# The last feed-forward of a twelve-stage decoder: every token through every expert, or tokens scattered to slots by expert

## The reference

```python
def _swiglu(flat, gate_w, up_w, down_w):
    return (silu(flat @ gate_w.T) * (flat @ up_w.T)) @ down_w.T
flat = x.reshape(-1, 128)                       # 1024 tokens, normalized
out = _swiglu(flat, shared_gate, shared_up, shared_down)      # 512 hidden channels
probs = softmax(flat @ router_w.T)              # 7 routed experts
top_vals, top_idx = top_k(probs, 2)
top_vals = top_vals / (top_vals.sum(-1) + 1e-9)
combine = sum(one_hot(top_idx, 7) * top_vals[..., None], axis=1)
for e in range(7):
    routed += combine[:, e:e+1] * _swiglu(flat, routed_gate[e], routed_up[e], routed_down[e])
return out + routed
```

## Time and profile before

| | |
|---|---|
| median of three runs | 1525.89 us (1523.6 to 1533.68) |
| profiled execution | 1525.1 us, span 1523.3 us |
| PE / DVE / ACT / POOL busy | 87% / 58% / 39% / 29% of the span |
| mean granted PE clock | 0.873 |
| last stage, first instruction to output issued | 1343.6 to 1520.2 us |
| HBM read / written | 91.15 MB / 1.59 MB |

### The profile page before, as it was taken

The page is one execution under the profiler, slowest core; times in us unless marked ns, Lnnn a source line. Parts: engine busy times, 40 slices in busy tenths (PEclk is TensorE's granted clock), DMA queues, the critical chain, the costliest instruction groups (busy, mean ns, idle before and its releaser), DMA issues. The chain is left out here.

```text
span 1523.3 us, 31521 instructions
## 1 busy us (share of the span) xinstructions
PE 1323.7 (87%) x12561; PEld 905.6 (59%) x12569; DVE 885.7 (58%) x1642; ACT 595.9 (39%) x1343; POOL 447.9 (29%) x251
## 2 busy tenths in 40 slices
PE   3579889989879898979997967979998998689998
PEld 1268878888745554556773554546674545356665
DVE  7488888888656645663335844861125767453333
ACT  2434444444325434514332711744435654122221
POOL 5099989999454031010002101110001010000000
PEclk9657888887877899979997977989997979789999
DMA  2197677877510000001110000000100000011110
GB/s 96 44 239 215 204 205 208 211 210 207 193 28 2 2 0 1 2 14 31 39 28 1 2 1 1 1 29 28 41 14 1 2 1 1 1 42 42 41 41 14
DMA packets 47097, 94.46 MB, mean 62 GB/s; under 512 B 4848, under 2 KB 9216, under 8 KB 46720
## 3 DMA queue, kind: packets, MB, share of 16 engines
q1 hardware_dynamic: 46976, 92.76, 21.8%
HBM read 91.15 MB, written 1.59 MB: 61 GB/s over the span
## 5 line engine op out<-in xcount | busy, mean ns | idle before, releaser
L618 ACT ACTIVATE shifted_a<-scores,nmax_a 128x128 f32<-128x128 f32 x768 | 208.6, 387 | 87.9 <-DVE nmax_a L584 86.5
L1078 PE MATMUL decay<-delta,A_pairs 32*128 32x127 f32 x2048 | 176.3, 333 | 47.3 <-DVE small_pack L1172 19.5
L1153 ACT ACTIVATE decay<-decay 128x1016 f32<-128x1016 f32 x128 | 128.7, 1010 | 193.8 <-PE decay L1078 193.8
L1410 DVE SCALAR_TENSOR_TENSOR X<-Y,comb_e,X 128x128 f32<-128x128 f32 x256 | 72.1, 345 | 212.0 <-PE Y L1352 212.0
L1334 PE MATMUL G<-XNT,W_e 128*128 128x512 f32 x384 | 193.3, 614 | 1.6 <-DMA W_e<-L3f_w 1.1
L1078 PEld LDWEIGHTS decay<-delta,A_pairs 32*128 32x128 f32 x2048 | 153.7, 233 | 67.7 <-DVE small_pack L1172 24.7
L1352 PEld LDWEIGHTS Y<-W_e,hid_e 128*128 128x128 f32 x1536 | 179.1, 192 | 23.0 <-issue 19.1
L584 DVE TENSOR_REDUCE nmax_a<-scores 128x4 f32<-128x512 f32 x192 | 123.8, 686 | 110.4 <-PE scores L523 108.1
L325 POOL TENSOR_TENSOR rstd<-ve,neghalf 128x4 f32<-128x4 f32 x30 | 30.6, 1022 | 520.0 <-DVE ve L311 520.0
L1352 PE MATMUL Y<-W_e,hid_e 128*128 128x128 f32 x1536 | 179.2, 275 | 0.0
L1377 ACT ACTIVATE hid_e<-G,W_e 128x512 f32<-128x512 f32 x128 | 88.0, 687 | 127.4 <-PE G L1334 122.6
(11 more groups left out here) (329 smaller groups left out, 2016.9 us busy)
## 6 DMA issues: line engine op xcount, KB each, us to landing
pos_bias<-du_rows SPq DMA_DIRECT2D x72, 256.0 KB, 4.8
XN<-du_rows SPq DMA_DIRECT2D x38, 256.0 KB, 4.7
XNT<-du_rows SPq DMA_DIRECT2D x38, 256.0 KB, 4.8
O<-du_rows SPq DMA_DIRECT2D x36, 256.0 KB, 4.7
masked_cos<-du_rows SPq DMA_DIRECT2D x36, 256.0 KB, 4.7
masked_sin<-du_rows SPq DMA_DIRECT2D x36, 256.0 KB, 4.7
W_e<-L3f_w SPq DMA_DIRECT2D x8, 768.0 KB, 4.2
small_pack<-small SPq DMA_DIRECT2D x1, 4517.0 KB, 14.4
```

What stands on the lines that cost most here:

```text
L618: t = nc.scalar.activation(shifted[u % 4][:, j, :], scores[u % 4][:, j, :], ACT.Exp, scale=-1.0, bias=nmax[:, u % 4, j:j + 1])
L1078: t = nc.tensor.matmul(decay[k % DEEP][:, s, i, 1:S], A_pairs[strip, c, 4 * q + i, :, :].rearrange("p j n -> p (j n)"), delta[strip, c, b ...
L1153: nc.scalar.activation(x, x, ACT.Exp).then_inc(decayed, 1)
L1410: nc.vector.scalar_tensor_tensor(out=x, in0=Y[s % 2][:, b, :], scalar=comb[:].rearrange("p b e -> p (b e)")[:, bass.ds(at, 1)], in1=x, op0 ...
```

## The change

`ffn3_stage` calls a new function, `sparse_stage`. The shared expert is computed densely, as before. For the routed ones, each token is copied twice, once for each of its experts, into rows of a DRAM tensor of slots, ordered by expert, each expert's rows beginning at a multiple of 128. 7 + (2048 - 7) // 128 = 22 blocks of 128 slots hold any routing, and always 22 are computed.

The slot numbers come from a one-hot table of the choices (bf16, 128 columns), two PE matmuls that count (all rows; earlier rows), and a row of DVE steps. POOL then scatters `XN` with 16 indirect DMAs of 128 rows of 512 bytes. SP loads the slots back in six groups of up to four blocks, PE turns them, DVE copies them to `XT`. For each block SP reads the expert's number from SBUF into a register and fetches its 768 KB of weights into one of three buffers. A block is four matmuls into G, four into U and four into Y, all of 128 columns. Unweighted results go to a second DRAM tensor; after the last store POOL gathers them with 16 indirect DMAs of 128 rows, DVE adds them to `X`, each with its token's weight, and SP stores the output in two halves.

The slots are filled with zeros in the early block, so that unused ones hold numbers. `Route` makes the one-hot table in place of `comb` here.

```diff
+            sp.wait_ge(zeros_ready, 1)
+            sp.dma_start(m.dram["slots_x"].rearrange("(j p) d -> p j d", p=128), bcast_mid(m.zeros[:], MOST_BLOCKS)
+                         ).then_inc(m.slots_zeroed, 16)
...
+            nc.gpsimd.memset(m.zeros[:], 0.0).then_inc(zeros_ready, 1)
+            nc.gpsimd.memset(m.onesb[:], 1.0)
+            m.pool_steps.done(pool, nc.gpsimd.memset(m.run_on[:], 1.0))
+            nc.gpsimd.memset(m.run_on[:, 0:16 * 16].rearrange("p (e g) -> p e g", g=16)[:, :, 0], 0.0)
...
+            nc.gpsimd.tensor_scalar(m.not_earlierb[:], m.w("causal"), 0.0, -1.0, ALU.is_gt, ALU.add)
...
+            if self.onehot is not None:
+                for k in range(2):
+                    v["onehot"] = steps.inc(nc.vector.tensor_tensor(
+                        self.onehot[:].rearrange("p e (k b) -> p k b e", k=2)[:, k], bcast_mid(m.w("iota16")[:, 0:EP], B),
+                        bcast_last(indexf[:, :, k], EP), ALU.is_equal))
...
+def sparse_stage(nc, m, layer, routed, FC, kind, func, weights, source, rows=(), b2=None, gated=False, last=False,
+                 residual=None, affine=None):
...
+    NB = E + (2 * T - E) // 128
+    GROUPS = [range(q, min(q + 4, NB)) for q in range(0, NB, 4)]
...
+    DEEP, UPS, HIDS = 3, (2 if gated else 3), 3
+    TURNS = 2 if gated else 1
+    BESIDE = 2 * FC if gated else 0
...
+            def fetch(j):
+                if j >= DEEP:
+                    sp.wait_ge(downed, j - DEEP + 1)
+                e = sp.value_load(expert_i[0:1, j:j + 1], min_val=0, max_val=E - 1)
+                sp.dma_start(W[j % DEEP][:], weights[bass.ds(e, 1)].squeeze(0)).then_inc(w_loaded[j % DEEP], 16)
+
+            def store(q):
+                js = GROUPS[q]
+                sp.wait_ge(y_copied, q + 1)
+                out = slots_y[js[0] * 128:(js[-1] + 1) * 128, :].rearrange("(j p) d -> p j d", p=128)
+                sp.dma_start(out, ys[:, js[0]:js[-1] + 1, :]).then_inc(y_stored, 16)
+
+            if gated:
+                sp.dma_start(shared[:], weights[E]).then_inc(shared_loaded, 16)
+            sp.wait_ge(listed, 1)
+            for j in range(DEEP):
+                fetch(j)
+            sp.wait_ge(scattered, 16 * 16)
+            for q, js in enumerate(GROUPS):
+                rows = slots_x[js[0] * 128:(js[-1] + 1) * 128, :].rearrange("(j p) d -> p j d", p=128)
+                sp.dma_start(xs[:, js[0]:js[-1] + 1, :], rows).then_inc(slots_loaded[q], 16)
+            stored = 0
+            for j in range(DEEP, NB):
+                fetch(j)
+                if j % 4 == 3 and j >= 7:
+                    store(stored)
+                    stored += 1
+            for q in range(stored, len(GROUPS)):
+                store(q)
+            if last:
+                for half in range(2):
+                    sp.wait_ge(combined, 4 * half + 4)
+                    sp.dma_start(m.dram["out"][:, halves[half], :], m.X[:, halves[half], :]).then_inc(m.stored, 16)
...
+            pool.wait_ge(m.slots_zeroed, 16)
+            pool.wait_ge(placed, 1)
+            for b in range(B):
+                for k in range(2):
+                    g = k * B + b
+                    nc.gpsimd.indirect_dma_start(slots_x, bass.IndirectOffsetOnAxis(ap=slot_i[:, g:g + 1], axis=0),
+                                                 source[:, b, :], None).then_inc(scattered, 16)
+            pool.wait_ge(y_stored, 16 * len(GROUPS))
+            for b in range(B):
+                for k in range(2):
+                    g = k * B + b
+                    nc.gpsimd.indirect_dma_start(back[:, g, :], None, slots_y,
+                                                 bass.IndirectOffsetOnAxis(ap=slot_i[:, g:g + 1], axis=0)
+                                                 ).then_inc(gathered[b], 16)
...
+            def turn(q):
+                pe.wait_ge(slots_loaded[q], 16)
+                if q >= TURNS:
+                    pe.wait_ge(turned_copied, q - TURNS + 1)
+                for j in GROUPS[q]:
+                    t = nc.tensor.transpose(turned_ps[q % TURNS][:, j % 4 * 128:(j % 4 + 1) * 128], xs[:, j, :],
+                                            m.w("ident"))
+                t.then_inc(turned, 1)
+
+            def up(j):
+                u = BESIDE + j
+                pe.wait_ge(w_loaded[j % DEEP], 16 * (j // DEEP + 1))
+                pe.wait_ge(turned_copied, j // 4 + 1)
+                if u >= UPS:
+                    pe.wait_ge(hidden, u - UPS + 1)
+                x = XT[:, j * 128:(j + 1) * 128]
+                for fc in range(FC):
+                    at = slice(fc * 128, (fc + 1) * 128)
+                    t = nc.tensor.matmul(G[u % UPS][:, at], W[j % DEEP][:, at], x, start=True, stop=True)
+                for fc in range(FC if gated else 0):
+                    at = slice(fc * 128, (fc + 1) * 128)
+                    t = nc.tensor.matmul(U[u % UPS][:, at], W[j % DEEP][:, F + fc * 128:F + (fc + 1) * 128], x,
+                                         start=True, stop=True)
+                t.then_inc(up_done, 1)
+
+            def to_down(j):
+                q = j // 4
+                pe.wait_ge(hidden, BESIDE + j + 1)
+                if j % 4 == 0 and q >= 2:
+                    pe.wait_ge(y_copied, q - 1)
+                for fc in range(FC):
+                    t = nc.tensor.matmul(four(Y[q % 2])[:, j % 4, :], hid[j % HIDS][:, fc, :],
+                                         W[j % DEEP][:, down + fc * 128:down + (fc + 1) * 128],
+                                         start=(fc == 0), stop=(fc == FC - 1))
+                t.then_inc(downed, 1)
+
+            def shared_up(u):
+                half, fc = u // FC, u % FC
+                if u >= UPS:
+                    pe.wait_ge(hid_ready, u - UPS + 1)
+                for ps, at in ((G, fc * 128), (U, F + fc * 128)):
+                    t = nc.tensor.matmul(ps[u % UPS][:], shared[:, at:at + 128], m.XNT[:, cols(half)], start=True,
+                                         stop=True)
+                t.then_inc(up_done, 1)
+
+            def shared_to_down(half):
+                pe.wait_ge(hid_ready, FC * (half + 1))
+                for b in range(B // 2):
+                    for fc in range(FC):
+                        t = nc.tensor.matmul(four(Y[half])[:, b, :], shared_hid[half][:, fc, b * S:(b + 1) * S],
+                                             shared[:, down + fc * 128:down + (fc + 1) * 128],
+                                             start=(fc == 0), stop=(fc == FC - 1))
+                t.then_inc(shared_down, 1)
+
+            if gated:
+                pe.wait_ge(shared_loaded, 16)
+                for u in range(UPS):
+                    shared_up(u)
+            pe.wait_ge(steps.sem, route.onehot_value)
+            chosen = onehot[:].rearrange("p e g -> p (e g)")
+            nc.tensor.matmul(rank[:, 0:N], m.onesb[:], chosen, start=True, stop=True)
+            nc.tensor.matmul(rank[:, N:2 * N], m.not_earlierb[:], chosen, start=True, stop=True).then_inc(ranked, 1)
+            if gated:
+                for u in range(UPS, 6):
+                    shared_up(u)
+                shared_to_down(0)
+                for u in range(6, 2 * FC):
+                    shared_up(u)
+                shared_to_down(1)
+                pe.wait_ge(begun, 2)
...
+            turn(0)
+            for j in range(NB):
+                up(j)
+                if j % 4 == 1 and j // 4 + 1 < len(GROUPS):
+                    turn(j // 4 + 1)
+                if j >= 1:
+                    to_down(j - 1)
+            to_down(NB - 1)
...
+                for u in range(BESIDE + NB):
+                    act.wait_ge(up_done, u + 1)
+                    if u >= 2:
+                        act.wait_ge(hid_ready, u - 1)
+                    nc.scalar.activation(silu[u % 2][:], G[u % UPS][:], func).then_inc(acted, 1)
...
+            dve.wait_ge(ranked, 1)
+            steps.done(dve, nc.vector.tensor_tensor_scan(seen[:], m.run_on[:, 0:N], rank[:, 0:N], 0.0, ALU.mult, ALU.add))
+            steps.done(dve, nc.vector.scalar_tensor_tensor(
+                out=count[:], in0=bcast_mid(iota, EP), scalar=128.0, in1=bcast_last(seen3[:, :, 15], 16), op0=ALU.mult,
+                op1=ALU.is_lt))
+            steps.done(dve, nc.vector.tensor_reduce(blocks[:], count[:], AX.X, ALU.add))
+            steps.done(dve, nc.vector.tensor_tensor_scan(ends[:], m.run_on[:, 256:256 + EP], blocks[:], 0.0, ALU.mult,
+                                                         ALU.add))
+            steps.done(dve, nc.vector.tensor_tensor(first[:], ends[:], blocks[:], ALU.subtract))
+            steps.done(dve, nc.vector.scalar_tensor_tensor(
+                out=place[:], in0=bcast_last(first[:], 16), scalar=128.0, in1=seen3, op0=ALU.mult, op1=ALU.add))
+            steps.done(dve, nc.vector.tensor_tensor(
+                place[:], place[:], rank[:, N:2 * N].rearrange("p (e g) -> p e g", g=16), ALU.add))
```

(66 more changed lines are left out.)

136 lines of the change are left out of this document (added).

## The result

The changed kernel takes 1520.05 us (median of 18 runs) against 1526.53 for the kernel before on the same chips: a ratio of 0.995, 95% interval 0.9936 to 0.9964. The gain is 6.5 us where the forecast had 21; the time lies in the range, and by the forecast's own bound of one per cent this is no change, to which it gave 0.31. The profiled execution took 1521.4 us, 3.7 less than that of before, with a span of 1519.6.

The account below looks back on a forecast made before the run. It took the stage as PE-bound at the upper clock: 87 us saved on PE, less 32 for blocks, 11 for the wait for slots and 24 for the tail, a difference of -20, forecast 1505 us, range 1482 to 1538.

Parts of the forecast that it names:

- PE's saving: Last stage: seven routed experts, 146 us of PE, replaced by 22 blocks of 2.68, 59 us; gain by PE work 87 us.
- the head: Last stage, from start of the logits to first G of a block: 40.4 us.
- the blocks: 22 blocks, first G to last Y: 11 us for the first two, then 10 turns, 80; together 91 us.
- Routing: Head: ranks at about 1355.1 behind two shared units, DVE steps 3.3 us at most, slots placed at 1358.4.
- Scatter and gather: Two rows of 16 indirect DMAs on POOL, 1.2 us each, 19.2 us a row, chosen between 0.35 and 2.45.
- the tail: After the last block: copy, store, 16 gathers, landing, additions and output; 27.7 us instead of 4.1.
- The POOL rival: POOL's indirect DMAs bind: at 1.9 us each the kernel takes 1527, at 2.45 it takes 1545; chance 0.24.
- Early part: Zeroed slots and masks in the early block: 0 us, at most 2 if they push POOL's power back.
- Latency of a turn: Blocks: register read 1.0, semaphores 0.15 and fetch landing 4.2 us, 5.35 in each turn of two blocks.
- Work in a turn: Blocks: 2.68 us of PE work added to the 5.35, making a turn of 8.03 us for two blocks.
- The clock rival: Clock falls between turns: blocks at 1.2 GHz need 5.36 us each, 118 instead of 91, kernel 1532; chance 0.13.
- The wait for slots: Head, 1348.3 to 1384: forecast 35.7 us; over 35 us was named as a sign of being wrong.

Follow-up runs that it names:

- 5: The kernel before plus only the early part of the change (memset, masks, 2 MB of zeros), old last stage: 1526.83 us, ratio 0.9997 to the kernel before.
- 9: The changed kernel with five weight buffers and one shared up unit instead of two ahead of the rank matmuls: 1480.49 us, ratio 0.9704 to the kernel before.
- 6: The changed kernel without the register read, block j fetching expert j mod 7: 1509.06 us, ratio 0.987 to the kernel before.
- 8: The changed kernel with 8 of the 16 gathers and the second expert's term left out: 1526.13 us, one run.
- 12: The changed kernel with 8 of the 16 gathers and the second expert's term left out, measured again: 1509.04 us, ratio 0.9888 to the kernel before.

## Why the prediction was wrong, step by step

- **PE's saving**: 87 us of matmuls at the upper clock; the page shows 62 less busy. The rate was right (four matmuls, eight records, in 0.89 us at the upper clock), but the granted clock averaged 0.79 in the head and 0.85 in the blocks, against 0.97 in the last stage before.
- **Routing**: slots placed at 1358.4 plus the late start of 3.9 is 1362.3; 1362.6 was measured. The shared weights landed in 5.4 us, not 4.2, but the clock rose sooner in the two units behind them, and the ranks came at 1359.2, where 1359.0 was due.
- **Scatter and gather**: 1.2 chosen between 0.35 and 2.45; measured 1.25 to 1.27. The choice by kind of work held, and with it the tail. The head's 1.5 is 0.3 of routing, 1.9 of scatter (0.9 between the slots' cast and the first issue, the rest 16 x 0.06), 0.5 of reading back (3.1 us from issue to transposes), less 0.3 of landing and 0.7 between transposes and first G, to within the rounding. The POOL rival, with 0.24, did not come.
- **Early part**: 0, and 5 shows none.
- **Latency of a turn**: 1.0 + 0.15 for the read and 4.2 for the fetch, 5.35. Measured 0.74, of which the read is 0.71, and 4.0 to 4.8 for the fetch: 5.2 on average. The sum was right, the read's 1.0 too much.
- **Work in a turn: the step that failed.** "With 0.15 for semaphores a turn is 5.35 + 2.68 = 8.03 us for two blocks" took G, U and Y at 2.4 GHz. The profile has 4.6 us for them in the turn shown, and turns of 9.55 on average (1401.0 to 1487.0 in nine). Nine turns of 1.5 more make 13.7 us. The stretch before them took 11.5 for the forecast's 11, and the last block 5.5, as nothing is fetched behind it, where the forecast counted a tenth whole turn; this slip hid 2.5 us by luck. Together that is the 12 of the table. The first turn, in which the clock stayed at 1.00, took 7.84 against the forecast's 8.03. With the clock held throughout, the turns are 8.6 and the blocks 93.7: 9.3 of the 12 are the clock, and the forecast misses the other 2.7. The transposes are in no term of the blocks (0.44 us at 1.00 in four of the nine turns, up to twice that at 0.50).
- **The clock rival** had the right mechanism and too small a chance, 0.13; its size, 1532, was too large. It took all PE work of the blocks at 1.2 GHz; in fact the clock fell in eight turns of ten, stood at 0.50 for about a third of each of these, and rose again while PE worked without a break. The evidence I set against it, the 1.00 from 1003 with PE busy 1.34 of 3 us, was a row of one stretch without its history, and the same group held the row that spoke for it. The Trainium skill (TensorE: Matmul & The Clock Gate, HAM oscillation) describes a loop whose short work is throttled again at every wait of about 3 to 5 us for the next operand. The trace agrees in the pattern and not in the numbers: here the waits were 2.1 to 2.8 us, and the clock fell behind eight of ten.
- **Against the median**: the profiled execution's gain of 3.7 is smaller than the medians' 6.5; its last stage began 3.9 us later. Without those the miss is 12.7, nearly all of it the blocks.

The signs I named to prove myself wrong included the granted clock at 0.5 within the blocks, and it was there. The wait for slots was over 35 us, too (1352.99 to 1389.49, 36.5), but that sign was badly set: the forecast itself had 35.7.

## What to carry to other kernels

When a change replaces one long run of matmuls by short ones with waits between them, price the work behind each wait at both clock levels, above all where that work is what the next transfer waits for: then the clock loss lies on the loop and is paid in each turn in which the clock falls, here eight of ten. One more buffer, so that the fetch no longer follows the compute, removes wait and clock loss at once (36 us here), while work put in the wait only keeps the clock (9.3). And price a row of indirect DMAs by their count, 1.25 us each on POOL: what can be covered, as the scatters were by the shared expert, is nearly free, and what stands alone, as the gathers do, is paid in full.

## What was not expected of the hardware

- Waits of 2.1 to 2.8 us, one in some 9.5 us, were enough for the granted clock to fall to 0.50 behind eight of ten. In 9, 0.55 us more of idle before the transposes came with a longer stretch at 0.50 in the first blocks; one execution, so the cause is open.
- In two of the profiled executions (6 and 8) DVE and ACT stood still in the head, some 7 us after the products that they were due to read had ended, and POOL went on issuing. From 8's timeline, and the stretch before:

```profile
1388.00:1391.00 3.00, 0.00 (x0) 0.00 (x0) 0.00 (x0) 0.00 (x0) 1.98 (x3) 1.00 0.13 44
...
1391.30 0.69 DVE L1778 TENSOR_TENSOR X<-X,Y_s 128x512 f32<-128x512 f32 x1 [9.68 <-remote]
```

  Both heads are 6.8 us longer for it, and both last stages had begun late (1352.5 and 1354.3). The releaser is given as "remote", and what it was stays open; 12, the same kernel as 8, did not have it.
- SP's register read with its bookkeeping is 0.71 us between a semaphore and the DMA behind it (0.74 against 0.03).
